# Fusing of weights put into the end of the first phase, routing counts by two products, own semaphores for loads, experts unrolled

## The chip, the cores and the metric

The kernel runs on one core of one Trainium2 chip. The metric is the device time in microseconds (us) of one execution of the whole program. TensorE is called PE, VectorE DVE, ScalarE ACT, GpSimd POOL and SyncE SP, as in the profile.

## The reference, cut to what matters

x is 64 x 128 tokens of width 256, ctx is 64 x 128 x 192. All is float32.

```
x = x + xattn0(layernorm(x), ctx, mask)          # 16 heads
n = layernorm(x)
probs = softmax(n @ w_switch + b_switch)         # 8 experts
route = argmax(probs); pos = cumsum(one_hot) - 1 # place in the expert's queue
keep = pos < 512                                 # capacity
h = relu(buf[e] @ w1[e] + b1[e]); y = h @ w2[e] + b2[e]
x = x + where(keep, y[slot], n) * (pmax / pmax)
x = x + xattn1(layernorm(x), ctx)                # 16 heads, then a 2-layer ffn
x = x + cell(layernorm(x))                       # below
```

The cell has six nodes. Node c takes q, k and v from earlier nodes, each through an edge matrix and a projection: q = ew[c,0] * (node @ We[e] + be[e]), then q @ Wq[c], and so for k and v. Then attention with 8 heads, and node[c] = act_w[c] * (o @ Wo[c]) + q. Since We[e] @ Wq[c] does not depend on the tokens, the kernel computes such products once: 18 of them (six nodes, three kinds). This is the fusing of weights.

## The kernel before, in words

The program has five blocks, with a barrier of all engines between them.

1. A block that loads the constants (L1396 to L1400).
2. `phase_first_layer` (L94): the first cross attention, the layernorm, the routing, and the scattering of rows to the experts' buffer in HBM. It works on 32 jobs of two batch rows (256 tokens). The order of the work on each engine is written out by hand as a table (L71 to L87): an entry `name:s` is the piece `name` of job k - s in step k. One step does a piece of up to ten jobs. In the DVE table `r.sh`, `r.oh` and `r.n^` are the routing; they and PE's `r.n` run for the last job of a group of four jobs (8 tiles) seven times, and for two groups of two jobs (4 tiles) at the end. `rs1` on POOL is the inverse square root for the second layernorm, `nm1` on DVE the normalising that waits for it. `put` on POOL (L283) sends the rows of a job by two indirect DMAs, at step j + 9; those of jobs 24 to 31 all come after the last work of POOL.
3. `phase_experts` (L599): a loop of four turns of two experts each. For an expert SP loads the rows, w1, w2, b1 and b2 with one semaphore `got` (L646 to L652); PE waits for all five (L659), turns the rows (8 transposes, L663), multiplies with w1 (L671), ACT applies relu (L692), PE multiplies with w2 (L680), DVE adds b2 (L715), and ACT's queue stores.
4. `phase_fuse` (L738): the 18 products. For each job SP loads two matrices of 256 KB into a ring of three places (L782, L783), PE computes the bias column (8 matmuls, L801) and the product (8 matmuls, L805), DVE scales it into `cell_w` (L814). Twelve plain matrices come by ACT's queue and are scaled at the end (L822, L824).
5. `phase_second_layer` (L869): the rest, with hand-written orders too. The change leaves its code alone.

In the first phase SP issues the loads of weights in one semaphore `w_in`, and both PE (L470) and DVE (L368) wait for all six of them before their first piece of work; the mask is loaded whole and widened to all partitions (L238). The routing counts how many tokens went to each expert before each token. PE's part (L588 to L593) for a group of w tiles is w products with a matrix of ones for the running total, one with a triangular matrix for the place inside a tile, and w - 1 with ones for the tiles before. DVE then adds the running total (L450, L451).

## Time and profile before

| | us |
|---|---|
| median of 3 runs | 4303.83 (4300.75 to 4309.98) |
| the profiled execution, its own time | 4306.31 |
| its span, first to last instruction | 4304.0 |
| PE busy | 4065.9 (94%) |
| DVE busy | 2511.5 (58%) |
| ACT busy | 2646.6 (61%) |
| POOL busy | 1754.8 (41%) |
| mean granted clock of PE | 0.978 of full speed |

PE is the busiest engine over the whole span. In the page's 40 slices its digit is 9 except in slices 0 (7), 6 (6), 8 (8), 9 (6) and the last (7): the dips are the start, the end of the first phase, and the end of the experts with the fusing. PEclk is the clock granted to PE in tenths of full speed. "Idle before" is the time that an engine stood still before an instruction, with what released it.

### The profile page before, as it was taken

The page shows a single profiled execution, that of the slowest core. Times are in us where ns is not written, and L with a number is a line of the kernel's source. Part 1 is how long each engine was busy: PE and PEld are TensorE (multiplying, and loading weights), DVE is VectorE, ACT ScalarE, POOL GpSimd, SP SyncE. Part 2 cuts the span into 40 slices and gives each one's busy share as a digit, 9 for nine tenths or more (in the row PEclk, how much of TensorE's full clock was granted, in tenths as well). Part 3 has the DMA queues.
Part 4 walks back from the last instruction along what each step waited for, and adds up shares of the span by engine and source line. Part 5 has one row for each costly group of instructions (what it writes and reads, how often), then busy time and mean ns, then how long its engine had stood idle before and what let it go on. Part 6 is the DMA issues. An engine that isn't in the chain of part 4 may idle for free.

```text
span 4304.0 us, 101370 instructions
## 1 busy us (share of the span) xinstructions
PE 4065.9 (94%) x38496; PEld 3449.7 (80%) x38496; DVE 2511.5 (58%) x6253; ACT 2646.6 (61%) x11818; POOL 1754.8 (41%) x1864
## 2 busy tenths in 40 slices
PE   7999996986899999999999999999999999999997
PEld 6888884664788888888888888888888888888885
DVE  6878871013566666666666666666666566666553
ACT  7878871211566666666666666666666666666663
POOL 4556651001344444444444444444444444444332
PEclk9999997997999999999999999999999999999998
DMA  3222112332000000000000000000000000000000
GB/s 111 65 63 72 60 46 94 116 111 89 18 14 16 14 14 13 13 13 14 13 13 13 21 13 15 11 12 12 12 12 12 11 12 11 19 11 14 4 4 6
DMA packets 116244, 129.66 MB, mean 30 GB/s; under 512 B 11926, under 2 KB 110596, under 8 KB 115136
## 3 DMA queue, kind: packets, MB, share of 16 engines
q1 hardware_dynamic: 102016, 107.53, 7.8%
q0 software_dynamic: 6144, 8.43, 0.7%
q10 hardware_dynamic: 7616, 7.34, 0.5%
q8 instruction: 308, 5.05, 0.5%
q14 instruction: 160, 1.31, 0.1%
HBM read 89.68 MB, written 41.94 MB: 31 GB/s over the span
## 4 chain that ended last, share of the span: by engine, by line
PE 58%; DVE 8%; ACT 5%; POOL 3%; issue 1%; DMA 0%; SPq 0%; POOLq 0%; DVEq 0%
PE c_product L1262 26%; PE c_product L1273 12%; PE c_product L1313 8%; PE c_scores L1303 6%; ACT c_front_probs L1083 4%; PE c_product L1336 4%; DVE c_neg_max L1138 2%; DVE c_xn L1123 2%; PE c_product L1324 1%; DVE c_routed L1123 1%; DVE c_x L1148 1%; POOL c_rstd L1029 1%; ACT c_probs L1083 1%; POOL c_probs L1041 1%; POOL c_front_probs L1041 1%
## 5 line engine op out<-in xcount | busy, mean ns | idle before, releaser
L1083 ACT ACTIVATE c_probs<-c_scores,c_neg_max 128x128 f32<-128x128 f32 x3072 | 1082.0, 407 | 480.6 <-DVE c_neg_max L1138 480.6
L1041 POOL TENSOR_TENSOR c_probs<-c_probs,c_row_inv 128x512 f32<-128x512 f32 x768 | 790.4, 1041 | 1211.0 <-DVE c_row_inv L1141 1208.3
L1262 PE MATMUL c_product<-c_nodes,cell_w 128*128 128x256 f32 x4352 | 1057.1, 383 | 2.9 <-DVE c_nodes L1129 1.2
L1262 PEld LDWEIGHTS c_product<-c_nodes,cell_w 128*128 128x128 f32 x4352 | 803.8, 191 | 124.8 <-issue 19.5
L1138 DVE TENSOR_REDUCE c_neg_max<-c_scores 128x4 f32<-128x512 f32 x1024 | 635.3, 682 | 255.2 <-PE c_scores L1303 255.2
L1083 ACT ACTIVATION_READ_ACCUMULATOR c_probs<-c_scores,c_neg_max 128x1 f32 x3072 | 758.3, 247 | 0.0
L1089 ACT COPY c_probsT<-c_product 128x512 f32<-128x512 f32 x768 | 413.3, 613 | 440.3 <-PE c_product L1313 440.3
L1083 ACT ACTIVATE c_front_probs<-c_scores,c_neg_max 128x128 f32<-128x128 f32 x1024 | 358.3, 403 | 188.5 <-DVE c_neg_max L1138 188.5
L1273 PE MATMUL c_product<-cell_w,c_nodes 128*128 128x256 f32 x1792 | 435.4, 383 | 0.0
L1313 PE MATMUL c_product<-consts_sb,c_probs 128*128 128x128 f32 x3072 | 398.7, 276 | 15.5 <-POOL c_probs L1041 14.4
L1313 PEld LDWEIGHTS c_product<-consts_sb,c_probs 128*128 128x128 f32 x3072 | 350.8, 142 | 48.6 <-POOL c_probs L1041 20.5
L311 ACT ACTIVATE a_probs<-a_scores,a_neg_max 128x128 f32<-128x128 f32 x1024 | 358.4, 404 | 46.1 <-DVE a_neg_max L377 46.1
L1273 PEld LDWEIGHTS c_product<-cell_w,c_nodes 128*128 128x128 f32 x1792 | 332.8, 190 | 49.0 <-issue 0.2
L1041 POOL TENSOR_TENSOR c_front_probs<-c_front_probs,c_row_inv 128x512 f32<-128x512 f32 x256 | 262.4, 1044 | 263.4 <-DVE c_row_inv L1141 263.4
L277 POOL TENSOR_TENSOR a_probs<-a_probs,a_row_inv 128x512 f32<-128x512 f32 x256 | 264.6, 1040 | 211.3 <-DVE a_row_inv L380 211.3
L1262 PE MATMUL c_product<-c_oT,cell_w 128*128 128x256 f32 x1280 | 328.8, 379 | 0.0
L1141 DVE RECIPROCAL c_row_inv<-c_row_sum 128x4 f32<-128x4 f32 x1024 | 167.3, 168 | 254.8 <-ACT c_probs L1083 178.6
L1262 PEld LDWEIGHTS c_product<-c_oT,cell_w 128*128 128x128 f32 x1280 | 243.0, 190 | 33.8 <-DVE c_oT L1129 1.0
L1129 DVE TENSOR_SCALAR c_qT<-c_product,cell_b 128x256 f32<-128x256 f32 x384 | 166.3, 474 | 147.7 <-PE c_product L1262 147.7
L311 ACT ACTIVATION_READ_ACCUMULATOR a_probs<-a_scores,a_neg_max 128x1 f32 x1024 | 250.2, 244 | 0.0
L1083 ACT ACTIVATION_READ_ACCUMULATOR c_front_probs<-c_scores,c_neg_max 128x1 f32 x1024 | 249.1, 243 | 0.0
L1129 DVE TENSOR_SCALAR c_kT<-c_product,cell_b 128x256 f32<-128x256 f32 x384 | 167.1, 477 | 130.4 <-PE c_product L1262 127.0
(158 smaller groups left out, 6551.5 us busy)
## 6 DMA issues: line engine op xcount, KB each, us to landing
e_w<-in_L_ffn_w SPq DMA_DIRECT2D x16, 1024.0 KB, 8.3
a_x<-in_x SPq DMA_DIRECT2D x32, 256.0 KB, 3.4
a_ctxT<-in_ctx_pairsT SPq DMA_DIRECT2D x32, 256.0 KB, 3.4
x<-a_x SPq DMA_DIRECT2D x32, 256.0 KB, 2.1
xn<-a_xn SPq DMA_DIRECT2D x32, 256.0 KB, 2.2
c_routed<-xn SPq DMA_DIRECT2D x32, 256.0 KB, 2.8
c_x<-x SPq DMA_DIRECT2D x32, 256.0 KB, 3.1
c_ctxT<-in_ctx_pairsT SPq DMA_DIRECT2D x32, 256.0 KB, 2.6
```

Of the source, the lines that this page charges most:

```text
L277: nc.gpsimd.tensor_tensor(p, p, rinv[:, j % 2, b, r].unsqueeze(2).broadcast_to([P, 4, T]), ALU.mult).then_inc(norm_made, 1)
L311: a = nc.scalar.activation(pr[:, j % 2, b, r, k], S[r][:, k], ACT.Exp, bias=nmax[:, j % 2, b, r, k:k + 1], accum_out=rsum[:, j % 2, b, r, ...
L1041: nc.gpsimd.tensor_tensor(e, e, rinv[:, i, r].unsqueeze(2).broadcast_to([P, 4, T]), ALU.mult).then_inc(norm_made, 1)
L1083: a = nc.scalar.activation(probs(n)[:, r, k], S[r][:, k], ACT.Exp, bias=nmax[:, i, r, k:k + 1], accum_out=rsum[:, i, r, k:k + 1])
L1089: nc.scalar.copy(probsT(n)[:, int(n[-1])], bank(n, j)[:]).then_inc(pT_made, 1)
L1129: k = V.tensor_scalar(dst[:, u], m[:, u], bias[:, u:u + 1], scalar, ALU.add, *([then] if then else []))
L1138: V.tensor_reduce(nmax[:, i, r], S[r][:], AX.X, ALU.max, negate=True).then_inc(max_made, 1)
L1262: i = T_.matmul(m[:, u], w[:, k, u * P:(u + 1) * P], src[:, k], start=n == 0, stop=n == last)
L1273: i = T_.matmul(m[:, b], src[:, k, b * T:(b + 1) * T], w[:, k], start=n == 0, stop=n == len(steps) - 1)
L1303: i = T_.matmul(S[r][:, k], q[e, u, b * T:(b + 1) * T], w[e, u, b * T:(b + 1) * T], start=True, stop=True)
L1313: i = T_.transpose(m[:, k], probs(name)[:, r, k], ident)
L1336: i = T_.matmul(m[32 * r:32 * r + 32, u, b * T:(b + 1) * T], va[:, group(c), b, h:h + 32], pT[:, group(c), r, k], start=True, stop=True)
```

## The change

- The block for the constants is gone. Constants, wk, wq, the mask of the first four jobs, w_switch and b_switch are issued on ACT's queue at the start of the first phase; wv and wo on SP's. Each has a semaphore of its own, and PE waits for each where it first needs it. The mask comes in pieces of four jobs, in a ring of two.
- The zeroing of the buffer uses 16 transfers from a tile of 512 columns, in place of 4 from 2048 columns. That tile is the fusing ring's first place.
- The ring of normalised rows has 8 places in place of 9.
- Routing counts: DVE keeps, after `r.oh`, a table `before` of one-hot sums, tile by tile (one addition of 128x8 per tile, each waiting for the one before). PE's `r.n` is two products over all tiles, triangular and ones. DVE no longer adds a running total.
- Fusing: pieces `F0` to `F17` (product) and `B0` to `B17` (bias column) stand in PE's order after the last pieces of the first phase, and `F^`, `B^` in DVE's. A ring of three places stays; SP issues the load of job n when `B{n-3}` is done. The first three jobs, the small tables, the twelve plain matrices and w1 of expert 0 are issued after the load of job 4. The plain matrices are scaled on POOL (`w.s`, two operations of 128x512 and one of 128x2), one node per step in steps 6 to 11, between `S1.n2` and `rs1`.
- Experts: unrolled. Rows, w1 and w2 have semaphores of their own, b1 and b2 come whole at the start. The rows of expert e + 1 are turned between the w1 and the w2 product of expert e, into the second of two places.
- `phase_fuse` is gone.

```diff
 FIRST_POOL_ORDER = """
-S0.n1:1 S0.n2:1 S0.n3:1 S1.n0:1 S1.n1:1 S1.n2:1 rs1:2 S1.n3:1 put:9 rs:-1 S0.n0:0
+S0.n1:1 S0.n2:1 S0.n3:1 S1.n0:1 S1.n1:1 S1.n2:1 w.s:6 rs1:2 S1.n3:1 put:9 rs:-1 S0.n0:0
 """
+FUSE_PE_PLACES = """
+T0.1:0 F0
+T1.1:0 B0 F1
+Tn:1 B1 F2
+L:1 B2 F3 F4 B3
+Tn:0 B4 F5
+L:0 B5 F6 F7 B6 B7
+r.n:0 F8 F9 B8 B9 F10 F11 B10 B11 F12 F13 B12 B13 F14 F15 B14 B15 F16 F17 B16 B17
+"""
+FUSE_DVE_PLACES = """
+nm1:1 F0^ B0^ F1^
+Tn^:1 B1^ F2^
+st1:0 B2^ F3^
+nm1:0 F4^ B3^
+Tn^:0 B4^ F5^
+r.sh:0 B5^ F6^
+r.oh:0 F7^ B6^ B7^
+r.n^:0 F8^ F9^ B8^ B9^
...
+"""
...
             load(0)
-            sp.dma_start(mku[:], mask.rearrange("b t -> (b t)").partition_broadcast(P)).then_inc(m_in, 16)
...
+            sp.dma_start(wv[:], halves(io["L0_xattn_Wv_rows"])).then_inc(wv_in, 16)
+            sp.dma_start(wo[:], halves(io["L0_xattn_Wo"])).then_inc(wo_in, 16)
...
+                if j == 4:
...
+                    for c in range(NODES):
+                        sp.dma_start(fw[:, c, EDGE], halves(io["L1_ffn_We"][plan[c]["edge"][0]])).then_inc(plain_in, 16)
+                        sp.dma_start(fw[:, c, OUT], halves(io["L1_ffn_Wo"][c])).then_inc(plain_in, 16)
+                    sp.wait_ge(buf_zeroed, 16 * parts.shape[0])
+                    for n in range(RING):
+                        fuse_load(n)
+                    sp.dma_start(w1_first[:], halves(io["L0_ffn_w1"][0])).then_inc(w1_in, 16)
...
+            for n in range(RING, len(fused)):
+                if n == 2 * RING:
+                    store(JOBS - 1)
+                sp.wait_ge(prod, n_prod[f"B{n - RING}", JOBS - 1])
+                fuse_load(n)
...
+                elif n == "w.s":
...
+                    for a, s in ((fw[:, c, EDGE], q), (fw[:, c, OUT], aw[:, c:c + 1])):
+                        nc.gpsimd.tensor_scalar(a, a, s, None, ALU.mult)
...
         def _(act):
+            act.dma_start(cst[:], io["consts"]).then_inc(consts_in, 16)
+            act.dma_start(wk[:], halves(io["L0_xattn_Wk_rows"])).then_inc(wk_in, 16)
+            act.dma_start(wq[:], halves(io["L0_xattn_Wq"])).then_inc(wq_in, 16)
+            act.dma_start(mku[:, 0], mask[0:2 * MASK_JOBS]...).then_inc(m_in[0], 16)
...
-                        V.tensor_tensor(oh[:, 0:w], over_t(i8[:]), over_e(route), ALU.is_equal).then_inc(hot, 1)
+                        chain(V.tensor_tensor(oh[:, 0:w], over_t(i8[:]), over_e(route), ALU.is_equal))
+                        for t in range(w):
+                            k = V.tensor_tensor(before[:, t0 + t + 1], before[:, t0 + t], oh[:, t], ALU.add)
+                            if t < w - 1:
+                                chain(k)
+                        k.then_inc(hot, 1)
...
-                    for t in range(w):
-                        T_.matmul(m[:, w * E:w * E + E], ones, oh[:, t], start=t == 0, stop=t == w - 1)
-                    T_.matmul(m[:, 0:w * E]..., tri, oh[:, 0:w], start=True, stop=False)
-                    for t in range(w - 1):
-                        i = T_.matmul(m[:, (t + 1) * E:w * E]..., ones, ...)
+                    T_.matmul(m, cst[:, C_TRI:C_TRI + P], oh[:, 0:t1 - t0], start=True, stop=False)
+                    T_.matmul(m, cst[:, C_ONE:C_ONE + P], before[:, t0:t1], start=False, stop=True).then_inc(prod, 1)
...
+            turn(0)
+            for e in range(E):
...
+                if e >= 1:
+                    pe.wait_ge(w1_in[s], ...)
+                pe.wait_ge(xT_made, 2 * e + 2)
...
+                if e + 1 < E:
+                    turn(e + 1)
+                pe.wait_ge(w2_in[s], 16 * (e // 2 + 1))
...
-        phase_fuse(nc, io, fw, fb, row5, cst)
```

## Rows read from the trace of the kernel before

**Rows 1.** Windows: stretch, us, busy per engine (PE, PEld, DVE, ACT, POOL), PEclk, DMA, GB/s
```profile
16.00:640.00 624.00, 592.28 (x7056) 509.45 (x7060) 491.88 (x1308) 514.60 (x2344) 367.34 (x429) 0.98 0.21 65
640.00:676.50 36.50, 14.50 (x120) 12.94 (x112) 10.83 (x48) 0.35 (x2) 17.50 (x19) 0.59 0.09 25
...
935.00:1007.40 72.40, 52.81 (x288) 47.66 (x288) 21.58 (x55) 0.00 (x0) 0.00 (x0) 0.81 0.57 177
1007.40:4304.00 3296.60, 3174.02 (x30208) 2725.51 (x30208) 1962.68 (x4800) 2086.43 (x9408) 1366.21 (x1410) 0.99 0.05 14
```

**Rows 2.** Timeline of 0 to 17: start, us, engine, line, operation, [idle before, releaser]
```profile
4.59 0.46 SPq L238 DMA_DIRECT2D a_mask_u<-in_mask_BxS_bf  x1
...
16.23 3.78 PE L506 MATMUL a_product<-a_ctxT,a_wk 128*128 128x256 f32 x8 [16.23 <-DMA a_b_switch<-in_L_ffn_b_switch]
16.26 0.69 DVE L384 TENSOR_SCALAR a_mask_add<-a_mask_u 128x1024 bf16<-128x1024 uint8 x1 [8.99 <-DMA a_b_switch<-in_L_ffn_b_switch]
```

**Rows 3.** DMA issues of 0 to 20: transfer, KB, median us to landing
```profile
a_mask_u<-in_mask_BxS_bf SPq DMA_DIRECT2D x1, 1024.0 KB, 8.2
```

**Rows 4.** Timeline of 300 to 316, PE: one routing step of the first phase
```profile
303.55 1.53 PE L546 MATMUL a_product<-consts_sb,a_probs 128*128 128x128 f32 x12 [1.52 <-POOL a_probs L277]
...
310.86 1.95 PE L589 MATMUL a_product<-a_one_hot,consts_sb 128*128 128x8 f32 x16
312.67 0.41 PE L590 MATMUL a_product<-a_one_hot,consts_sb 128*128 128x64 f32 x2
...
314.45 3.42 PE L506 MATMUL a_product<-a_ctxT,a_wk 128*128 128x256 f32 x8
```

**Rows 5.** Timeline of 640 to 692, DVE: two chained steps on small tiles
```profile
660.21 0.19 DVE L454 TENSOR_TENSOR a_place<-a_place,a_one_hot 128x32 f32<-128x32 f32 x1
660.43 0.19 DVE L455 TENSOR_REDUCE a_pos<-a_place 128x4 f32<-128x32 f32 x1
```

**Rows 6.** Windows at the clock, first phase (columns of group 1)
```profile
316.00:318.00 2.00, 2.00 (x7) 1.52 (x6) 0.09 (x1) 0.00 (x0) 0.00 (x0) 0.50 0.00 0
...
148.00:150.00 2.00, 2.00 (x19) 1.59 (x21) 1.08 (x2) 1.47 (x3) 1.81 (x3) 0.50 0.13 39
```

**Rows 7.** Timeline of 116 to 156, POOL: a gap ahead of the second square root
```profile
129.11 0.20 POOL L264 TENSOR_TENSOR a_var_eps<-a_mean_var,consts_sb 128x2 f32<-128x2 f32 x1 [1.10 <-DVE a_mean_var L347]
```

**Rows 8.** Groups by line and form, POOL, 100 to 600: xcount, busy, mean ns, idle before
```profile
L277 POOL TENSOR_TENSOR a_probs<-a_probs,a_row_inv 128x512 f32<-128x512 f32 x208 | 214.9, 1040 | 169.9 <-DVE a_row_inv L380 169.9
```

**Rows 9.** Groups by line and form, 935 to 1008
```profile
L805 PE MATMUL f_product<-f_w,f_edgeT 128*128 128x256 f32 x144 | 39.1, 419 | 0.0
...
L1032 POOL MEMSET c_v_even<- 128x512 f32 x1 | 0.5, 524 | 338.3 <-POOLq L749 338.3
```

**Rows 10.** Timeline of 640 to 692: end of the first phase, start of the experts
```profile
648.93 1.04 POOL L294 DMA_INDIRECT buf<-a_xn,slots  x1 [0.20 <-issue]
...
668.15 0.97 POOL L294 DMA_INDIRECT buf<-a_xn,slots  x1 [0.30 <-issue]
676.54 0.40 SPq L646 DMA_DIRECT2D e_rows<-buf  x1
...
687.33 1.96 PE L663 MATMUL e_turned<-consts_sb,e_rows 128*128 128x128 f32 x8 [27.45 <-DMA e_b<-in_L_ffn_b]
...
690.15 2.07 PE L671 MATMUL e_hidden<-e_rowsT,e_w 128*128 128x512 f32 x2 [0.86 <-DVE e_rowsT L710]
```

**Rows 11.** Timeline, PE: between the second and the third expert
```profile
749.65 1.04 PE L663 MATMUL e_turned<-consts_sb,e_rows 128*128 128x128 f32 x8
752.50 14.00 PE L671 MATMUL e_hidden<-e_rowsT,e_w 128*128 128x512 f32 x32 [1.82 <-DVE e_rowsT L710]
```

**Rows 12.** Timeline of 955 to 966, PE: bias columns of two jobs of the fusing phase
```profile
958.80 0.95 PE L801 MATMUL f_biases<-f_be,f_w 128*128 128x1 f32 x8
...
961.42 0.95 PE L801 MATMUL f_biases<-f_be,f_w 128*128 128x1 f32 x8
```

**Rows 13.** DMA issues of 955 to 1000: transfer, KB, median us to landing
```profile
f_w<-in_L_ffn_Wk SPq DMA_DIRECT2D x5, 256.0 KB, 3.1
```

More of the change, by code:

```diff
@@ L104, in phase_first_layer @@
     W2 = PAIR * T
-    X_RING, ROW_RING, GROUP = 4, 9, 4
-    MASK_JOBS, SENDS = 4, 3
+    X_RING, ROW_RING, GROUP = 4, 8, 4
+    MASK_JOBS, SENDS, RING = 4, 3, 3
+    plan = cell_plan()
+    NE = io["L1_ffn_We"].shape[0]
+    SCALE = 1.0 / np.sqrt(D // CELL_HEADS)
+    fused = [(c, k, plan[c]["edge"][k]) for c in range(NODES) for k in (TO_Q, TO_K, TO_V)]
     PAIRS_OF_HEADS = D // 32
@@ new lines, in turn @@
+            def turn(e):
+                pe.wait_ge(rows_in[e % 2], 16 * (e // 2 + 1))
+                for u in range(2):
+                    if e >= 1:
+                        pe.wait_ge(xT_made, 2 * e - 1 + u)
+                    for n in range(NR):
+                        i = nc.tensor.transpose(TB[u][:, n * P:(n + 1) * P], xr[:, e % 2, n, u * P:(u + 1) * P],
+                                                cst[:, C_ID:C_ID + P])
+                    i.then_inc(turned, 1)
+            turn(0)
@@ L698, in _ @@
+            act.wait_ge(b1_in, 16)
+            for e in range(E):
+                for c in range(HC):
+                    act.wait_ge(hid, e * HC + c + 1)
+                    nc.scalar.activation(hT[:, c], HB[c % HBANKS][:], ACT.Relu, bias=b1t[:, e, c:c + 1]).then_inc(hid_made, 1)
+                for q in range(YB):
+                    act.wait_ge(y_made, YB * e + q + 1)
+                    act.dma_start(dst[e, q], y[:, q]).then_inc(y_out[q], 16)
             for q in range(YB):
-                act.wait_ge(y_out[q], 16 * E + 16)
+                act.wait_ge(y_out[q], 16 * E)
@@ new lines, in rows_turned @@
+            def rows_turned(e):
+                for u in range(2):
+                    dve.wait_ge(turned, 2 * e + u + 1)
+                    nc.vector.tensor_copy(xT[:, e % 2, u], TB[u][:]).then_inc(xT_made, 1)
+            dve.wait_ge(b2_in, 16)
+            rows_turned(0)
+            for e in range(E):
+                if e + 1 < E:
+                    rows_turned(e + 1)
+                for q in range(YB):
+                    dve.wait_ge(out, YB * e + q + 1)
+                    if e >= 1:
+                        dve.wait_ge(y_out[q], 16 * e)
+                    nc.vector.tensor_tensor(y[:, q], Y[q][:], b2t[:, e].unsqueeze(1).broadcast_to([P, 2, D]),
+                                            ALU.add).then_inc(y_made, 1)
```

392 lines of the change are left out of this document (173 added, 219 removed).

## The prediction, made before the changed kernel was seen or run

> **What bounds the kernel now.** I read the page first, then windows cut at the phases, then timelines at each seam. The windows show a kernel that PE sets: 592.3 busy of 624 us in the first phase and 3174 of 3296.6 in the second layer, at a granted clock of 0.98 and 0.99 [rows 1]. The second layer is not touched, so its 3297 us stay. What the change can reach lies between: the start, PE's own work in the first phase, and the three seams. At the start PE and DVE stand until 16.2 for the sixth weight [rows 2]. At the end of the first phase PE is busy 14.5 us of 36.5, at clock 0.59 [rows 1], while POOL sends the last rows [rows 10]. Between SP's first load for the experts (676.54) and the first product with w1 (690.15) lie 13.6 us [rows 10]. The fusing phase takes 72.4 us by itself, 52.8 of them PE [rows 1].
>
> **The sum, part by part.** A minus is a gain.
>
> *Fusing phase gone: -72.4* [rows 1]. The experts' end and the second layer's first load then adjoin, with one barrier less.
>
> *Start: -8.* Before, the mask is issued at 4.59 and lands 8.2 us later as 1024 KB [rows 2, 3]; DVE starts with the mask at 16.26 [rows 2]. Now the mask is ACT's fourth issue, at 0.5 us each (an SP issue takes 0.46 [rows 2]) between 2.3 and 3.6, as 128 KB behind some 700 KB. If it takes between half and all of the old 8.2 us it lands at 6.4 to 11.8; I take 8, as there is an eighth of the bytes: DVE and PE start 8 us sooner. Range -4 to -10. The 16 zeroing transfers cost SP some 5 us more of issuing than four would, ahead of the load of job 2, which is a step away from its use: nothing.
>
> *Routing: -10.* A group of 8 tiles has its ones and triangle products from 310.86 until the next step's K product at 314.45: 3.6 us [rows 4]. Two products of the form of L590 remain, which took 0.25 us from start to next start; with issue gaps 0.5. PE is full here, so -3.1 per group. Against it stand eight chained additions on DVE after `r.oh`. Steps of that size follow each other by 0.22 us [rows 5], so 1.7 us. Queued behind them on DVE is `S1.i1`, behind that POOL's `S1.n1`, and PE's transposes wait just there already, 1.52 us [rows 4]: the wait grows by the full 1.7. Net -1.4 each, times seven: -10.
>
> Here the clock comes in. It fell to half (the 1.2 GHz level) once per group: after the 1.5 us wait in some groups (0.50 in 148 to 150), after the run of eight-column products in others (0.50 in 316 to 318) [rows 6]; the K product of eight matmuls then took 3.42 us [rows 4], nearly twice what it needs hot, so a fall costs some 1.7 us. The change shortens one cause and lengthens the other; I leave the falls as they are, with -12 to +6 for all seven. The Trainium skill (TensorE: Matmul & The Clock Gate, "HAM oscillation") says that PE waits between bursts put its clock back to cold; by that rule the longer wait takes the fall in all seven groups and the sum keeps its place. The trace agrees with it in part, since the run of small products was followed by a fall without any wait.
>
> *Plain matrices scaled on POOL: +4.* No row shows this operation on POOL. Below it is bounded by a fill of 128x512 (0.52 us [rows 9]), above by POOL's two-input multiplication of that size (1.04 us [rows 8]). I take 0.8: one tensor is read, not two. With the small one 1.8 us per node, in a gap of 1.1 us that POOL has there [rows 7]; the rest, 0.7, holds up `rs1`, `nm1` behind it on DVE and the next maxima. Six nodes: +4, ends 0 and +9.
>
> The Trainium skill (GPSIMD Engine Reference, "Performance versus the Vector engine") puts a one-input body at 1.03 cycles per element, as an estimate 0.44 us for 512. By that price the part costs nothing and the total would be 4 us lower; no row here shows it.
>
> *Loads after job 4: 0.* SP issues 23 transfers there, 11 us, and some 5.6 MB pass, at the fusing phase's 177 GB/s [rows 1] in 32 us, or less. Queued behind are `store(1)` and the loads of job 5, whose first user is a step (17 to 18 us) and more later. If that cover is gone, +10 once.
>
> *End of the first phase: +22.* PE now gets 18 fused jobs. A hot job took 2.62 us from bias column to bias column [rows 12]; 17.4 of them after 640 are 45.6 us. The old work there, 14.5 us at clock 0.59, is some 8.6 hot [rows 1]. So PE alone comes to 640 + 8.6 + 45.6 = 694.2. Then the ring: job n + 3 is loaded only after `B{n}`; the table runs F F B B from F8 on, so one of each pair waits. Issue 0.4, landing 3.1 [rows 13], a job 2.6, handover 0.1: 6.2 us per pair against 5.24. Four pairs: +4. PE ends at 698.2, against 676.54: +21.7. POOL's 16 sends (1.28 us each, 648.93 to 669.1 [rows 10]) begin some 3 us later, because F0, F1 and F2 stand ahead of the last output product; they end near 680 with landing, and are no longer the last.
>
> *First expert's start: -6.5.* The 10.8 us from first load to first transpose [rows 10] were the wait for five transfers. Now only the rows, 512 KB, are awaited. A 256 KB load lands in 3.1 [rows 13]; I take 4.2. w1 is there already. Ends -3 and -8.
>
> *Between experts: -13.* From the start of the transposes to the next w1 product 2.85 us pass [rows 11]; I take 2.8 for all. Moved ahead of the w2 product, the transposes cost 0.95 and DVE's copies are hidden under the w2 product. Ends: 0 (below) and -14. Seven times -1.85. Rows, w1 and w2 of an expert are asked for a whole expert ahead.
>
> Sum: -72.4 - 8 - 10 + 4 + 21.7 - 6.5 - 13 = -84. The profiled execution took 4306.3 (span 4304.0), so 4222; the median is 2.5 below it, and 4220 is what I forecast for a median.
>
> **The rivals.**
>
> *Faster, about 4204.* The fused jobs run at PE's pace (-4), POOL's scaling hides in its gap (-4), and with the small products gone most falls of the clock go too (-8). For it: small products alone were followed by a fall. Against it: the wait of 1.5 us grows to 3.2.
>
> *A cold, starved tail, about 4240.* The loads of the ring share the transfers with POOL's sends, PE stands in every pair, and the clock goes down. The old phase's matmuls took 419 ns on the mean, its cold first jobs included [rows 9]. At half clock a job takes up to 5.2 us, a pair 10.5 in place of 6.2; five pairs, most of them cold, add 18. For it: in 640 to 676.5 the clock stood at 0.59 [rows 1]. Against: the ring ran at 2.62 without a wait in the old phase [rows 12]. The Trainium skill's rule on the clock, named above, speaks for this rival.
>
> *Slower than before, above 4313.* One mechanism: POOL's scaling by a column is far slower than its two-input multiplication. Twelve operations lie in six steps, and PE waits behind each. With d us per operation a step loses 2d - 0.9; it must take back 84 + 4 + 9 = 97 us, so it decides from d = 8.5. Against: 0.52 and 1.04 for operations of this size [rows 8, 9].
>
> *A part doesn't do what it says, about 4233.* The transposes of the next rows wait for the rows or for a PSUM bank and the gap stays at 2.8. Against: the old schedule had loads two experts deep, too.
>
> **How the numbers follow.** Forecast 0.56, faster rival 0.17, cold tail 0.18, experts' gap stays 0.06, slower 0.02, no effect seen 0.01. A measurement here can tell about 0.2%, 8.6 us. The range takes in the faster rival, at 4200, and the cold tail, at 4243; what it leaves out is both ends' bounds together, about 2 in 10. All cases but the last two are faster by far more than 8.6 us.
>
> **What would show it.** Windows: the first K product near 8; the distance of K products around a routing group down by 1 to 2; the wait ahead of PE's twelve transposes 3.2 in place of 1.5. POOL's new groups: 0.8 each. PE's last B near 685 (14 us earlier than in my frame of before, since start, routing and scaling move it), then 7 us to the first w1 product; 28.6 us per expert; the second layer's first load near 923. It would be wrong if the last fused job ended before POOL's last send had landed, if PE stood for loads after job 4, or if the second layer's 3297 us moved by more than 5.

## The result and the profile after

| | before | after | ratio of the times, 95% interval |
|---|---|---|---|
| median of 4 executions, us | 4305.38 | 4260.67 | 0.9897 [0.9881, 0.9912] |
| span of the profiled execution, us | 4304.0 | 4260.1 | |
| granted clock over the span | 0.978 | 0.978 | |

The change is faster by 44.7 us, about half of the 84 us that were forecast, and 4260.67 lies outside the range of 4200 to 4243. The two spans differ by 43.9 us. Cut at places that both kernels have, they give the account below. The K product of a job is the first matmul of its step, so the distance of two K products is the time of the steps between.

| stretch | before | after | difference | forecast |
|---|---|---|---|---|
| start to the K product of job 2 | 47.3 | 43.9 | -3.4 | -8 |
| K product of job 2 to that of job 31 | 555.4 | 572.4 | +17.0 | -6 (routing -10, scaling +4) |
| K product of job 31 to SP's first load for the experts | 73.9 | 102.5 | +28.6 | +21.7 |
| that load to the first product with w1 | 13.6 | 13.1 | -0.5 | -6.5 |
| first w1 product to the next phase's first load | 244.9 | 231.8 | -13.0 | -13 |
| fusing phase | 72.4 | 0 | -72.4 | -72.4 |
| second layer | 3296.6 | 3296.4 | -0.2 | 0 |

The two largest terms that take time away, and the second layer, came out as forecast. Every term of the first phase and of the seam behind it came out worse. The windows of the kernel after, in the columns of [rows 1], cut at the K products of jobs 2, 6, 12 and 31 and at the experts' first load:

```profile
43.87:113.55 69.68, 68.77 (x857) 58.57 (x853) 56.91 (x147) 63.26 (x289) 39.26 (x48) 1.00 0.47 148
113.55:252.75 139.20, 116.09 (x1309) 98.04 (x1305) 98.70 (x271) 98.89 (x450) 88.38 (x99) 0.91 0.18 56
252.75:616.28 363.53, 341.51 (x4123) 294.28 (x4122) 300.06 (x808) 304.42 (x1384) 228.09 (x266) 0.97 0.21 65
616.28:718.76 102.48, 91.19 (x704) 79.13 (x700) 55.25 (x167) 29.88 (x136) 38.53 (x42) 0.91 0.31 95
```

The second stretch is the one to see: PE stands 23.1 of 139.2 us, and its granted clock is 0.91. The first one moves 148 GB/s, the loads asked for at job 4, at clock 1.00 and without a lost microsecond. The same cut of the kernel before, jobs 6 to 12:

```profile
116.88:237.80 120.92, 114.93 (x1365) 99.80 (x1361) 96.66 (x257) 100.19 (x460) 67.97 (x80) 0.97 0.20 62
```

Here is what stands in these steps. Hot means at the 2.4 GHz level of PE's clock. First POOL's groups by line and form in 113 to 253 us of the kernel after (line, engine, operation, shapes, count, busy us and mean ns, idle before), then from its timeline the step of job 6:

```profile
L374 POOL TENSOR_SCALAR cell_w<-cell_w,a_ew 128x512 f32<-128x512 f32 x6 | 9.4, 1570 | 0.0
L374 POOL TENSOR_SCALAR cell_w<-cell_w,a_act_w 128x512 f32<-128x512 f32 x6 | 9.3, 1558 | 0.0
L375 POOL TENSOR_SCALAR cell_b<-a_be,a_ew 128x2 f32<-128x2 f32 x6 | 1.7, 290 | 0.0
```
```profile
124.66 1.58 POOL L374 TENSOR_SCALAR cell_w<-cell_w,a_ew 128x512 f32<-128x512 f32 x1
126.22 1.56 POOL L374 TENSOR_SCALAR cell_w<-cell_w,a_act_w 128x512 f32<-128x512 f32 x1
...
130.07 0.66 PE L665 MATMUL a_product<-consts_sb,a_probs 128*128 128x128 f32 x4 [3.24 <-POOL a_probs L361]
130.56 3.12 PE L631 MATMUL a_product<-a_wv,a_ctxT 128*128 128x256 f32 x8
```

The scaling of one matrix takes 1.57 us where 0.8 was taken (between 0.52 and 1.04, [rows 8, 9]). PE waits 3.24 us behind it, and the product after that takes 3.12 us for eight matmuls that take 1.89 hot. A routing step, PE and DVE, timeline of 384 to 410:

```profile
394.90 1.57 DVE L564 TENSOR_TENSOR a_tokens_before<-a_tokens_before,a_one_hot 128x8 f32<-128x8 f32 x8
396.39 0.17 DVE L483 RECIPROCAL a_row_inv<-a_row_sum 128x4 f32<-128x4 f32 x1
```
```profile
397.73 2.82 PE L665 MATMUL a_product<-consts_sb,a_probs 128*128 128x128 f32 x12 [3.14 <-POOL a_probs L361]
...
406.44 0.43 PE L711 MATMUL a_product<-a_one_hot,consts_sb 128*128 128x64 f32 x2
406.71 0.39 PE L712 MATMUL a_product<-a_tokens_before,consts_sb 128*128 128x64 f32 x2
```

The wait ahead of the twelve transposes grew from 1.52 us [rows 4] to 3.14, as forecast, and the two products take 0.5 us, as forecast. But the transposes now run at the 1.2 GHz level: 2.82 us in six of the seven full groups, 1.81 in the other. Before, they took 1.53 [rows 4] in three groups and at most 2.35. Cut into windows of half a microsecond, PE stands at the 1.2 GHz level for 10 us of jobs 12 to 31 before the change and for 24 us after it.

Now the end of the first phase and the experts' start, timeline of 679 to 735, PE and SP:

```profile
679.66 5.38 PE L624 MATMUL a_product<-a_edge_w,a_edgeT 128*128 128x256 f32 x16
...
689.77 1.99 PE L624 MATMUL a_product<-a_edge_w,a_edgeT 128*128 128x256 f32 x8 [1.22 <-DMA a_edge_w<-in_L_ffn_Wv]
...
696.05 1.99 PE L624 MATMUL a_product<-a_edge_w,a_edgeT 128*128 128x256 f32 x8 [0.77 <-DMA a_edge_w<-in_L_ffn_Wk]
...
703.59 2.92 PE L624 MATMUL a_product<-a_edge_w,a_edgeT 128*128 128x256 f32 x8 [2.04 <-DMA a_edge_w<-in_L_ffn_Wq]
706.31 3.41 PE L726 MATMUL a_product<-a_be,a_edge_w 128*128 128x1 f32 x16
709.58 6.24 PE L624 MATMUL a_product<-a_edge_w,a_edgeT 128*128 128x256 f32 x16
...
722.80 1.97 PE L798 MATMUL e_turned<-consts_sb,e_rows 128*128 128x128 f32 x8 [5.29 <-DMA e_rows<-buf]
731.90 13.49 PE L814 MATMUL e_hidden<-e_rowsT,expert_w_first 128*128 128x512 f32 x27 [7.14 <-DVE e_rowsT L850]
```
```profile
718.76 0.37 SPq L773 DMA_DIRECT2D e_rows<-buf  x1
```

In three of the five pairs one load is awaited, 4.0 us in all; four such waits of 1.0 were forecast, so that the sums agree is in part luck. A pair with a wait takes 6.28 us (689.77 to 696.05; 6.2 forecast). After the third wait the clock falls: the two F products take 6.24 us instead of 3.70. It had fallen once before, in the first pair (5.38 us at 679.66), with PE busy up to it. From 679.66 to 717.5 the ten jobs take 37.8 us: 26.2 hot (ten times 2.62 [rows 12]), 4.0 of waits and 7.6 that are left. Of these, 6.7 are matmuls at the low clock, 1.7 in the first pair and 5.0 behind the third wait. The rows land 4.04 us after their load, 4.2 forecast, but then PE stands 7.14 us behind DVE's copy: DVE's first instruction in that phase waits for b2, the fourth load, of 1024 KB.

### The profile page after: what moved, and what is told of

Same layout as the page of the kernel before. It is cut to its first block, busy times and chain, and to the rows that moved or that the text cites. A ratio compares the mean times of both kernels' runs of the same rounds, so it can differ in the third digit from the quotient of the medians.

```text
span 4260.1 us, 100693 instructions
## 1 busy us (share of the span) xinstructions
PE 4052.2 (95%) x38276; PEld 3431.3 (81%) x38276; DVE 2515.5 (59%) x6280; ACT 2647.2 (62%) x11818; POOL 1774.9 (42%) x1883
## 4 chain that ended last, share of the span: by engine, by line
PE 58%; DVE 9%; ACT 5%; POOL 3%; issue 1%; DMA 0%; SPq 0%; POOLq 0%; DVEq 0%
PE c_product L1297 26%; PE c_product L1308 12%; PE c_product L1348 8%; PE c_scores L1338 6%; ACT c_front_probs L1118 4%; PE c_product L1371 4%; DVE c_neg_max L1173 2%; DVE c_xn L1158 2%; DVE c_routed L1158 1%; PE c_product L1359 1%; DVE c_x L1183 1%; POOL c_rstd L1064 1%; ACT c_probs L1118 1%; POOL c_probs L1076 1%; PE c_product L1285 1%
```

## The experiments

The theory from these two traces: each term was lost to one cause of its own, and each can be taken away alone. (a) POOL's scaling is slow and PE stands behind it; (b) the chained additions stand ahead of the reciprocal that POOL and PE wait for; (c) the wait for b2 stands ahead of the copies; (d) the order F F B B keeps the ring from being loaded; (e) the mask lands late. The rival to (a) is the traffic of job 4; to (b) and (d), a fall of the clock that comes whatever stands there; to (c) and (e), transfers that share the bandwidth. All experiments are edits of the changed kernel. In the table, the ratio is to the kernel before, run beside each; the stretches are from the profiled execution. A stretch is known only to some 3 to 4 us, for kernels with the same work in it differ by that much: the start to the K product of job 2 takes 40.9 to 44.0 us, jobs 6 to 12 take 116.1, 118.7 and 119.0 in scale_dve, clean_new and clean_shifted, jobs 12 to 31 take 359.6 to 363.5 in all kernels that leave the routing of the change as it is.

| kernel | median us | ratio, 95% | jobs 6 to 12 | jobs 12 to 31 | job 31 to experts |
|---|---|---|---|---|---|
| after | 4260.67 | 0.9897 [0.9881, 0.9912] | 139.2 | 363.5 | 102.5 |
| scale_dve | 4236.57 | 0.9841 [0.9825, 0.9858] | 116.1 | 362.9 | 100.9 |
| scale_two_input | 4255.89 | 0.9886 [0.9870, 0.9903] | 128.4 | 362.1 | 107.8 |
| adds_later | 4248.95 | 0.9871 [0.9855, 0.9888] | 135.1 | 354.7 | 100.9 |
| routing_spread | 4237.93 | 0.9851 [0.9835, 0.9868] | 138.6 | 344.7 | 101.5 |
| old_counts | 4273.11 | 0.9929 [0.9913, 0.9946] | 145.5 | 365.6 | 110.0 |
| b2_later | 4254.68 | 0.9881 [0.9865, 0.9898] | 139.2 | 363.5 | 102.5 |
| tail_alternated | 4250.20 | 0.9878 [0.9861, 0.9894] | 138.9 | 361.8 | 92.3 |
| start_early | 4267.04 | 0.9913 [0.9896, 0.9929] | 139.4 | 362.3 | 109.1 |
| clean_new | 4236.70 | 0.9843 [0.9827, 0.9859] | 118.7 | 359.6 | 103.9 |
| clean_old | 4250.02 | 0.9875 [0.9859, 0.9891] | 121.0 | 365.2 | 103.0 |
| clean_held | 4238.21 | 0.9841 [0.9825, 0.9858] | 118.7 | 359.6 | 108.2 |
| clean_shifted | 4234.36 | 0.9838 [0.9822, 0.9854] | 119.0 | 361.4 | 102.4 |
| combined | 4203.04 | 0.9765 [0.9749, 0.9782] | 108.2 | 345.8 | 98.2 |
| combined_warm | 4203.79 | 0.9764 [0.9748, 0.9781] | 108.3 | 345.8 | 98.3 |
| combined_shifted | 4204.65 | 0.9759 [0.9743, 0.9775] | 108.0 | 345.8 | 98.2 |

### The scaling on DVE: scale_dve

```diff
-S0.n1:1 ... S1.n2:1 w.s:6 rs1:2 ...            (POOL's order)
-r.n^:0 F8^ F9^ B8^ B9^ F10^ F11^ ...           (DVE's places)
+r.n^:0 F8^ F9^ W0 B8^ B9^ W1 F10^ F11^ W2 ...
+elif n[0] == "W":      # node c: V.tensor_scalar on fw[:, c, EDGE], fw[:, c, OUT], fb[:, c, EDGE]
```

> The changed kernel with the scaling of the plain matrices taken off POOL: the same twelve operations run on DVE among the last fused jobs, where DVE waits for PE. The loads after job 4 stay as they are. Theory (POOL's scaling by a column took 1.57 us each, 3.4 us per node, and PE stood 3.2 us behind it in steps 6 to 11): the distance of the K products of jobs 6 and 12 falls from 139.2 us back to about 121 (it was 120.9 before the change), PE's wait ahead of its transposes falls from 3.2 to 1.0 to 1.5, and the time falls by 16 to 20 us against the changed kernel, to about 4243. Rival (the 5.6 MB of loads asked for at job 4 hold these steps up, and POOL's wait is only where it shows): the distance stays within 3 us of 139 and the time within 4 us of 4261.

Measured: 116.1 us in jobs 6 to 12 instead of 139.2, and 24.1 us less by the medians, 29.8 by the spans, more than the theory's 16 to 20. PE's wait is 0.99 us again. The loads stayed as they were. The rival is out: PE stood behind POOL.

```profile
111.24:227.37 116.13, 106.97 (x1308) 92.10 (x1305) 97.44 (x267) 96.92 (x441) 66.47 (x79) 0.99 0.22 65
```

The windows also give the split. PE's idle time falls from 23.1 to 9.2 us (14.0) and its busy time from 116.1 to 107.0 (9.1), with the clock up from 0.91 to 0.99. So the six nodes cost 2.3 us each of waiting and 1.5 us each of clock. Against clean_new, where the same steps take 118.7 us, the whole is 20.5 instead of 23.1.

### Another form of the operation: scale_two_input

```diff
-nc.gpsimd.tensor_scalar(a, a, s, None, ALU.mult)
+nc.gpsimd.tensor_tensor(a, a, s.unsqueeze(2).broadcast_to([P, 2, D]), ALU.mult)
```

> The changed kernel with the plain matrices scaled on POOL in the same places, but by a multiplication with a broadcast second tensor in place of the operation with a factor per partition. Theory (the form of the operation makes it slow: 1.57 us by a factor per partition, 1.04 for a multiplication of two tensors of that size): the twelve operations take 1.04 to 1.1 each, POOL's insertion falls from 3.4 to 2.4 us a node, PE's waits in steps 6 to 11 from 3.2 to 2.2, and the time falls by 6 to 10 us. Rival (the matrix in place, or its two-part shape, makes it slow whatever the form): 1.5 to 1.6 each and no change beyond 3 us.

Measured, POOL's groups in 112 to 241 us:

```profile
L374 POOL TENSOR_TENSOR cell_w<-cell_w,a_ew 128x512 f32<-128x512 f32 x6 | 6.2, 1040 | 0.0
L374 POOL TENSOR_TENSOR cell_w<-cell_w,a_act_w 128x512 f32<-128x512 f32 x6 | 6.2, 1040 | 0.0
```

The same result of the same tile takes 1.04 us instead of 1.57 with a second tensor in place of a factor per partition. The form is slow, not the place. Jobs 6 to 12 became 10.8 us shorter; the median fell by only 4.8, short of the 6 to 10 expected, and the end of the phase took 5.3 us more. That loss comes back below.

### The additions moved: adds_later

```diff
-S1.i1:1 O^:2 S1.i2:1 L^:3 r.sh:3 st1:2 S1.i3:1 nm1:2        (r.oh:4 with the additions ahead)
+S1.i1:1 O^:2 S1.i2:1 L^:3 r.sh:3 st1:2 S1.i3:1 r.bf:4 nm1:2 (the additions are r.bf)
```

> The changed kernel with the eight chained additions of a routing group moved on DVE behind the step's last reciprocal, ahead of the normalization that waits for POOL. Theory (the additions, 1.6 us ahead of the reciprocal that POOL and PE wait for, doubled PE's wait to 3.1 us, and the clock then fell in every group): PE's wait ahead of the twelve transposes is 1.5 us again, the transposes take 1.5 in place of 2.8 in at least three of seven groups, the steps with a group shorten by 2 to 3 us, and the time falls by 12 to 20 us, to about 4245. Rival (a step with a group is long for another reason, such as the next group's work on DVE, and the two products gave all they could): the wait falls but the steps shorten by less than 1 us, and the time falls by less than 5.

Measured, PE, a full group:

```profile
389.31 2.82 PE L666 MATMUL a_product<-consts_sb,a_probs 128*128 128x128 f32 x12 [1.65 <-POOL a_probs L361]
```

The wait is back to 1.65 us, but the transposes still take 2.82 in five groups of seven and 2.72 in a sixth. Steps with a group take 21.2 us instead of 22.5 to 23.9. The time fell by 11.7 us, just short of the theory's 12 to 20. The half about the wait holds; the half about the clock does not: a wait of 1.65 us was enough for a fall.

### The routing's work spread over steps: routing_spread

```diff
-... r.n^:5 S1.x0:1 ... Tn^:3 r.oh:4 S1.i1:1 ... L^:3 r.sh:3 st1:2 S1.i3:1 nm1:2
+... r.n^:6 r.oa:4 r.ba:5 S1.x0:1 ... Tn^:3 S1.i1:1 ... L^:3 st1:2 S1.i3:1 r.sh:3 r.ob:4 r.bb:5 nm1:2
-V:0 A:1 r.n:4      (PE)
+V:0 A:1 r.n:5
```

> The changed kernel with a routing group's work on DVE spread over three steps: the shift and both halves of the one-hot ahead of the normalization or the maxima that DVE waits for anyway (0.8 to 1.2 us idle in each step), the additions in two halves a step later, PE's two products and the places one step later than now. Moving the additions alone took the wait ahead of the twelve transposes from 3.1 to 1.65 us, and the transposes still took 2.82 in six of seven groups. Theory (any wait above an ordinary step's one sets the clock back there, and the one-hot work in front of the reciprocal is the rest of it): the wait shrinks to 0.3 or less, the twelve transposes take 1.5 to 1.9 in all groups, and the steps with a group go from 22.5 to about 18, the steps after and before them from 18.2 and 18.5 to about 17.6: 5 to 6 us a group, 35 to 42 us in all, so about 4222. Rival (the clock falls once in each group whatever stands there, or DVE has no room elsewhere in its steps): the group's step stays above 20 us and the gain below 20.

Measured, windows of four steps, the first with a group's one-hot work:

```profile
376.16:394.06 17.90, 17.66 (x220) 14.98 (x217) 16.50 (x44) 15.17 (x69) 12.13 (x14) 1.00 0.26 75
394.06:413.33 19.27, 18.68 (x224) 15.37 (x221) 17.66 (x50) 17.44 (x83) 12.88 (x15) 1.00 0.24 79
413.33:431.49 18.16, 17.24 (x218) 14.81 (x217) 15.60 (x43) 15.59 (x72) 11.57 (x15) 1.00 0.20 67
431.49:448.84 17.35, 17.35 (x220) 15.03 (x216) 14.76 (x40) 15.95 (x74) 12.07 (x15) 1.00 0.20 63
```

The clock stays at 1.00 through the whole group; four steps take 72.7 us instead of 76.5 to 77.9. Over jobs 12 to 31, with the long steps of four groups, that is 18.8 us, 4.7 per group. The forecast of 5 to 6 was a little too high (the step after the group takes 19.3, not 17.6), and the two groups that lie in POOL's scaling gained nothing: 22.7 us in all, not 38. But the cause is settled: DVE's routing work stood in front of a reciprocal that PE waits for, and the clock went down with the wait.

### The old counts put back: old_counts, clean_old

The edit restores the running totals, their additions on DVE and the 16 products per full group.

> The changed kernel with the old routing counts put back: running totals in place of the tokens before a tile, so no chained additions on DVE, and the ones and triangle products, 16 of them per full group, on PE. Theory (the two products save 3.1 us per group on PE, but DVE's additions and the fall of the clock behind the longer wait give it back): a group's four steps take 77 to 78.5 us in place of about 76.5 to 78, and the time is higher by 0 to 5 us, 4261 to 4266. Rival (my forecast's term: the routing change is worth 10 us): 4269 to 4272.

> Three mendings together, the routing left as the change has it: the scaling on DVE in the tail, the wait for b2 behind the first copies, the last ten fused jobs alternated. Theory (the three costs lie in different stretches and add up: -29.8 for the scaling by its profile, -5.3 for b2, and in the tail from 100.9 to about 92.3 us between the last K product and the experts' first load): a span of about 4216 and a median within 4 us of it. Rival (part of what the tail or the scaling gave was one execution's or one layout's luck with the clock): 4222 to 4232.

> The same three mendings with the old routing counts put back (running totals, 16 products per full group, no chained additions), so that the routing change is weighed where no scaling on POOL and no starved tail lie over it. Theory (my forecast's term was nearly right in size: without the scaling the change's own steps gained 4.8 us in jobs 6 to 12 and 2.0 in jobs 12 to 31 over the kernel before): slower than the mended kernel with the new counts by 6 to 10 us. Rival (a wait of 3.1 us with a fall of the clock in each group eats it up): within 3 us of it.

In the changed kernel the old counts cost 12.4 us: the rival, my forecast's own term, holds better than the theory that I had formed from the two traces. But 7.5 us of that lie in the last stretch (110.0 against 102.5), and jobs 12 to 31 are longer by only 2.1. In the mended kernel they cost 13.3 by the medians and 9.8 by the spans. There the steps can be weighed: from the K product of job 2 to that of job 31 pass 548.0 us with the new counts and 555.9 with the old, where the kernel before takes 555.4. That is 7.9 us for six groups, 1.3 each, of the 1.4 that I had forecast (the long step of the seventh group is that of job 31 and lies in the last stretch). The start, which is the same in both, is 2.2 us shorter in clean_old, so that the places of the K product of job 31 (591.1 and 596.8) differ by 5.7 only; of the rest, 2.0 come at the first expert and 2.3 in the second layer. So the routing change as built is worth some 8 us in the steps, and moved off the reciprocal some 24 us more (clean_new against combined: 591.1 and 567.4 at the K product of job 31).

clean_new itself was a miss: 4236.70, where 4216 was expected. Its last stretch took 103.9 us, not 92.3. As in scale_two_input, this stretch ate a gain made elsewhere.

### The wait for b2: b2_later

```diff
-dve.wait_ge(b2_in, 16)
 rows_turned(0)
 for e in range(E):
     if e + 1 < E:
         rows_turned(e + 1)
+    if e == 0:
+        dve.wait_ge(b2_in, 16)
```

> The changed kernel with DVE's wait for the bias b2 moved from ahead of the first copy of turned rows to ahead of the first addition that reads it. Theory (DVE's copy, and with it PE's first w1 product, waited 7.1 us for the fourth load of the phase and for nothing else): from SP's first load of the phase to the first w1 product pass 6.5 to 7.5 us in place of 13.1, and the time falls by 5.5 to 7 us. Rival (the transfers that are issued together hold PE up anyway: the rows or w2 come late): the wait moves to the w2 product behind it, and the time falls by less than 2 us.

Measured, PE and SP's first load at 718.78:

```profile
722.88 1.97 PE L798 MATMUL e_turned<-consts_sb,e_rows 128*128 128x128 f32 x8 [5.36 <-DMA e_rows<-buf]
725.63 17.07 PE L814 MATMUL e_hidden<-e_rowsT,expert_w_first 128*128 128x512 f32 x32 [0.78 <-DVE e_rowsT L850]
```

6.85 us from the load to the product, as the theory has it, and 6.0 us less by the medians. All K products are where they were to 0.2 us, so this one difference stands alone up to there; the experts behind it take 1.4 us more (233.2 against 231.8). The intervals of the ratios overlap.

### The order of the last jobs: tail_alternated

```diff
-r.n:0 F8 F9 B8 B9 F10 F11 B10 B11 ...
+r.n:0 F8 B8 F9 B9 F10 B10 F11 B11 ...
```

> The changed kernel with the last ten fused jobs in the order product, bias column, product, bias column, where the table had two products and then two bias columns, so that each ring buffer is loaded again at once. Theory (one job of each pair waited for its load, 0.8 to 2.0 us, and the clock fell behind the longest wait and at the start of the tail): the waits of 1.22, 0.77 and 2.04 us go, 4 us, and of the 6.8 us that slow matmuls cost there at least 2.5 (those behind the last wait): from the first of these jobs (679.66) to the end of the last bias column 32 us in place of 37.8, the time lower by 5 to 8 us. Rival (loads take longer than a job however they are asked for, since SP issues four of them in a row and POOL's sends share the transfers): waits stay, the time falls by less than 2 us.

Measured, PE:

```profile
694.65 0.95 PE L726 MATMUL a_product<-a_be,a_edge_w 128*128 128x1 f32 x8
695.46 1.97 PE L624 MATMUL a_product<-a_edge_w,a_edgeT 128*128 128x256 f32 x8
697.27 0.95 PE L726 MATMUL a_product<-a_be,a_edge_w 128*128 128x1 f32 x8
```

Every one of the ten jobs takes 2.62 us, no wait is left and no slow product: the stretch fell by 10.2 us, the median by 10.5, more than expected. The low clock behind the third wait went with the waits. The one in the first pair, which had no wait ahead of it, went too; no run here takes these two apart.

### The start: start_early, combined_warm

```diff
 act.dma_start(cst[:], ...)
+act.dma_start(mku[:, 0], ...)          # was the fourth
 ...
 act.wait_ge(consts_in, 16)
+nc.scalar.activation(warm[:], cst[:, C_HALF:C_HALF + 2], ACT.Exp)
```

> The changed kernel with the mask's first rows issued second instead of fourth on ACT, and a two-element activation ahead of ACT's first work, so that the activation table is loaded before it (in the changed kernel the load took one of the two waits of the first activation and ran at 14.52, 1.28 us, between DVE's and ACT's halves of the keys). Theory (the start is bounded by DVE's wait for the mask at 10.24): DVE begins with the mask at 6 to 7, the first Q product starts at 11.5 to 12.5 in place of 15.73, and the second K product (23.94) some 3.5 to 4.5 us earlier; the time falls by as much. Rival (the transfers of the start share the bandwidth, so that what the mask gains the first rows of x or the first weights lose): the Q product moves by less than 1.5 us.

Measured, timeline of 0 to 24:

```profile
7.71 0.69 DVE L488 TENSOR_SCALAR a_mask_add<-a_mask_u 128x1024 bf16<-128x1024 uint8 x1 [2.29 <-DMA a_mask_u<-in_mask_BxS_bf]
...
9.88 3.75 PE L625 MATMUL a_product<-a_ctxT,a_wk 128*128 128x256 f32 x8 [9.88 <-DMA a_wk<-in_L_xattn_Wk_rows]
...
15.26 3.78 PE L625 MATMUL a_product<-a_xT,a_wq 128*128 128x256 f32 x8 [0.78 <-DVE a_xT L495]
```

The rival holds. The mask lands 2.5 us sooner, wk 4.1 us later, and the Q product starts 0.5 us sooner (15.73 in the kernel after), the second K product 1.2 us. The median is 6.4 us higher, and the trace has that in the last stretch again: 109.1 us.

combined_warm has the two-element activation without the new order of loads.

> The same with a two-element activation ahead of ACT's work, so that the activation table is loaded while ACT waits for nothing else; the order of the first loads stays. Theory (the table's 1.28 us lie between DVE's and ACT's halves of the keys at 14.5, but the first scores wait for the Q product, which ends at 19.5, so nothing is gained): the first scores start within 0.5 us of the other kernel's and the time is within 3 us of it. Rival (that path does hold the first scores up): 1 to 1.5 us sooner.

DVE's first maximum starts 0.87 us sooner (21.09 against 21.96), 0.64 of which the mask's landing gives; the medians are 0.75 us apart. The table's load is beside the path, as expected.

### All together: combined

scale_dve, b2_later, tail_alternated and routing_spread in one (the scaling stands among the last jobs in their new order).

> The three mendings and the routing's work on DVE spread over three steps. Theory (with the scaling gone from POOL, the spreading works in all seven groups, not in five: four steps take 72.7 us in place of 76.5 to 78): faster than the three mendings alone by 24 to 32 us, a time of about 4188. Rival (DVE becomes the limit in more steps once POOL's delays are gone): 4196 to 4205.

4203.04 us, faster than clean_new by 33.7 (the spans by 29.7: 23.7 by the K product of job 31, 5.7 in the last stretch). It beats both kernels: 0.9765 [0.9749, 0.9782] of the kernel before. The absolute time missed 4188, since clean_new had missed 4216. It lies in the rival's range, but not for the rival's reason: jobs 12 to 31 take 345.8 us, as in routing_spread (344.7), and jobs 6 to 12 take 10.5 us less than in clean_new.

### What the last stretch hangs on: clean_held, clean_shifted, combined_shifted

In clean_new, DVE, and POOL's twelfth send of an unbroken row that began at 644.30:

```profile
654.47 0.17 DVE L534 TENSOR_TENSOR a_logits<-a_product,a_b_switch 128x16 f32<-128x16 f32 x1 [3.57 <-PE a_product L623]
...
660.14 0.22 DVE L529 TENSOR_SCALAR cell_b<-a_product,a_ew 128x2 f32<-128x2 f32 x1 [5.05 <-remote]
```
```profile
658.45 0.97 POOL L378 DMA_INDIRECT buf<-a_xn,slots  x1 [0.30 <-issue]
```

PE had done its part: the product that the first reads was issued at 648.66, the one that the second reads at 649.47, and PE went on to the two products behind them. SP waits for the same bias column on the same semaphore (`prod`, for `B5`) before its next load for the ring, and it goes on in the same moment as DVE:

```profile
649.47 1.03 PE L725 MATMUL a_product<-a_be,a_edge_w 128*128 128x1 f32 x8
...
660.14 0.37 SPq L276 DMA_DIRECT2D a_edgeT<-in_edgesT  x1
```

In the changed kernel SP's load follows the start of `B5` by 1.07 us (673.77 behind 672.70), here by 10.67. DVE and SP go on together, within 0.02 us, in clean_shifted, combined, scale_two_input and start_early too, 3.7 to 9.9 us later than those 1.07. So DVE doesn't stand for a reason of its own: PE's signal, product made, reaches two engines late. That the profile calls the releaser "remote" proves little, for it does so at an ordinary wait for the scores, too (2.53 us at 610.28). PE, its clock and POOL's last four sends then wait for DVE.

> The kernel with the three mendings, with POOL's last sixteen sends held back until the bias column of the eighth fused job, so that the stretch in which DVE stood (650.9 to 660.1, ended with POOL's twelfth send) runs without sends. Theory A (DVE's standing is bound to POOL's sends, in which instructions or data of DVE don't get through): DVE's waits of 3.6 and 5.1 us there are gone, or move into the new stretch of sends; the last K product to the experts' first load takes 92 to 96 us in place of 103.9. Theory B (DVE waits for its own program to be fetched, at a place of the program, whatever POOL does): both waits stay where they are, and the stretch takes 100 or more.

> The kernel with the three mendings and 48 one-column fills on DVE ahead of its first work, where it waits for the mask anyway, so that every later instruction of DVE stands 48 places further on. Theory B (a fetch at a place of the program): the waits of 3.6 and 5.1 us on DVE move to other operations, or fall where DVE has nothing to do; the stretch takes anything from 92 to 104. Theory A (POOL's sends, whatever the place in the program): the same two waits ahead of the same two operations (the sums of the logits and the bias column of the sixth fused job), and the stretch takes 103 to 105.

> The fastest kernel so far (three mendings, routing spread) with the same 48 fills. Theory B: DVE's 2.2 us ahead of the sums of the logits and PE's 4.3 us behind it move or go, and the stretch from the last K product to the experts' first load (98.2) changes by 2 us or more, to either side. Theory A: within 1 us of 98.2, time within 2 us of 4203.

```diff
+if j == JOBS - ROW_RING:                       # clean_held, POOL, ahead of a put
+    pool.wait_ge(prod, n_prod["B7", JOBS - 1])
+for r in range(48):                            # the shifted ones, DVE, ahead of its first work
+    V.memset(pad[:, r:r + 1], 0.0)
```

clean_shifted, DVE:

```profile
653.96 0.17 DVE L537 TENSOR_TENSOR a_logits<-a_product,a_b_switch 128x16 f32<-128x16 f32 x1 [2.23 <-remote]
...
660.28 0.22 DVE L532 TENSOR_SCALAR cell_b<-a_product,a_ew 128x2 f32<-128x2 f32 x1 [5.69 <-remote]
```

The same two operations, with 48 more instructions ahead of them; the stretch, 102.4 us, is just below theory A's 103 to 105. combined_shifted has its stall of 2.19 us in the same place too, and its stretch is 98.2 us, as in combined. Theory B is out. In clean_held the sends run from 656.45 to 676.85, DVE:

```profile
670.80 0.22 DVE L531 TENSOR_SCALAR cell_b<-a_product,a_ew 128x2 f32<-128x2 f32 x1 [3.55 <-PE a_product L625]
...
679.29 0.75 DVE L516 TENSOR_SCALAR cell_w<-a_product,a_ew 128x512 f32<-128x512 f32 x1 [7.16 <-remote]
```

The stalls moved with the sends, to other operations, and grew. SP's loads go on with DVE again (670.79 and 679.37). The stretch took 108.2 us, not theory A's 92 to 96, which had left out what the stalls cost in their new place. So they hang on a long row of POOL's sends, and the last of them ends where the row ends (0.7 us after it in clean_new, 2.4 in clean_held). Such a row is not enough, though: the changed kernel has sixteen sends in a row, 667.54 to 687.7, and tail_alternated another, and neither shows a stall. The Trainium skill (SBUF — State Buffer, "SBUF: two separate sides") says that DVE and GpSimd share one pair of ports under an exclusive lock, which counts for a DVE operation in a two-port mode or with two inputs from SBUF, so that the loser stands. That could hold DVE up, but not SP, which stood just as long; and the same operations of DVE ran beside sends elsewhere at their usual 0.2 and 0.75 us. Why PE's signal comes late beside a row of sends stays open.

## Why the prediction was wrong, step by step

*Fusing phase gone, between experts, second layer:* right: -72.4, -13.0 and -0.2 against -72.4, -13 and 0. *Loads after job 4:* right at 0; 43.87 to 113.55 takes 69.68 us, and took 69.61 before.

*Plain matrices scaled on POOL, +4:* this step failed most: 23.1 us, 19 more than forecast (20.5 against clean_new). It had two faults. The price: "I take 0.8: one tensor is read, not two"; it is 1.57, above both ends. I had taken the two-input multiplication for an upper bound with no row that says so, and the range's end of +9 came from it. With 1.57 my own formula of the slower rival (2d - 0.9, 2.24 us per step) gives 13.4, and the idle time did grow by 14.0. So the path was right. The second fault: no clock in the term. Behind the waits of 3.2 us PE ran at the 1.2 GHz level for a while (granted clock 0.91 against 0.99 over these steps), 9.1 us more. The Trainium skill's price (GPSIMD Engine Reference, "Performance versus the Vector engine", 1.03 cycles per element for a body of one or two operations, 0.44 us as an estimate) is further off still; the measurement decides.

*Routing, -10:* the two parts were right (3.1 off PE, 1.6 us more of a wait), and in the mended kernel so is the term: -7.9 us for the six groups that lie ahead of the K product of job 31, where 6 times -1.4 is -8.4. In the changed kernel it was mis-sized by some 4 us: 17.0 less 23.1 leaves -6.1, and jobs 12 to 31 gained only 1.3 us over four groups. PE's idle time grew there by 6.9 us, as forecast, but its busy time fell by 8.2, not by the 12.7 of clean_new. The step that failed is "I leave the falls as they are": PE stands at the 1.2 GHz level for 24 us of this stretch, against 10 before. In clean_new, with the same wait of 3.13 us, it is 10 us as before, and one group of seven has no fall at all; what decides between the two no run here shows. ("Once per group" was too many as well: before the change the clock had fallen in five of the six groups.) Without the wait it does not fall at all: combined has no such window in jobs 2 to 31. The Trainium skill's rule (TensorE: Matmul & The Clock Gate, "HAM oscillation"), which I had weighed and set aside for the sum, holds in part: in the changed kernel the transposes behind the wait ran slow in six groups of seven, in clean_new in four of seven.

*End of the first phase, +22:* 28.6, so 6.9 us off. Pairs of 6.28 us, waits of 4.0 us and POOL's sends out of the way were as forecast (6.2, 4, not last), the sum of the waits in part by luck. The clock was not: 6.7 us of slow matmuls, for which the term had nothing. This is the cold tail's mechanism at under half its price of 18. I had given it 0.18 as a rival; part of it belonged in the forecast, since the same rule speaks of waits of just the kind that I had counted.

*First expert's start, -6.5:* -0.5. "Now only the rows, 512 KB, are awaited" is false for DVE. The diff shows `dve.wait_ge(b2_in, 16)` ahead of `rows_turned(0)`; I had followed PE's and SP's waits and not DVE's. b2_later gives 6.3 us back: the size was right, the step was missing one wait.

*Start, -8:* -3.4 in this profile; with the same loads in the same order, the kernels tried reach the K product of job 2 between 40.9 and 44.0 us, so -3.3 to -6.4. The mask landed at 10.24, inside my bounds of 6.4 to 11.8, but I had taken 8. DVE is 6.0 us sooner, and PE, which has stood 4.3 us between the K product and the next work, then takes 3.78 us for the Q product against 1.99 before.

The errors all have one sign: 4.6 + 19.1 + 3.9 + 6.9 + 6.0 = 40.5 us, which is the miss but for 0.2 in the second layer. The ranges of the terms were treated as if their faults were independent. But about half of it has one cause: waits cost twice here, once as idle time and once through the clock (9.1 at the scaling, some 4 at the routing, 6.7 in the tail), and this was left out of every term. The other half is POOL's price (14.0 of idle time where 4 were forecast), the wait for b2 and the start.

## What to carry to other kernels

Price an operation that no row shows by more than its operand count: on POOL a factor per partition was half as dear again as a second tensor, and a bound needs a row of its own kind. Where a matmul engine is full, a wait that grows from 1 or 1.5 us to 3 costs its own length and up to 1.5 us again through the clock (from nothing in clean_new to 1.5 per step at the scaling), so look for slots in which the in-order engine ahead of it waits anyway (here: split the work over three steps, 22 us). When waits are moved between phases, follow them on every engine's queue, since one early `wait` ahead of a copy cost what the new loads had won.

## What was not expected of the hardware

- POOL takes 1.57 us for 128x512 with a factor per partition and 1.04 for a two-tensor multiplication of that size, in place, in the same steps.
- A first activation with two waits in front: the activation table's load (1.28 us) took the first of them and ran at 14.52 instead of in the idle time before, timeline of the kernel after:

```profile
14.52 1.28 ACT L425 ACT_TABLE_LOAD   x1 [14.52 <-DVE a_kT_even L499]
15.73 3.78 PE L624 MATMUL a_product<-a_xT,a_wq 128*128 128x256 f32 x8 [0.78 <-DVE a_xT L494]
```

  It lay beside the path, so it cost nothing here.
- In a long row of POOL's indirect sends, PE's signal that a product is made can reach DVE and SP 4 to 10 us late, both in the same moment; the waits of DVE that come of it are 2 to 7 us. They move with the sends and not with the place in DVE's program. Kernels that show them have a last stretch up to 12 us longer (103.9 us in clean_new, 92.3 in tail_alternated, which differ in DVE's scaling too). Not every such row brings it, and the cause is not shown.
